# Moving the residual add of a graph-attention layer from VectorE to GpSimd, with a new order on all engines

## The chip, the cores and the metric

One core of a Trainium2 chip runs the whole program. The metric is the device time of one execution in microseconds (us). Five engines work side by side, each through its own instructions in order: TensorE (PE in the profile; its weight loads are PEld), VectorE (DVE), ScalarE (ACT), GpSimd (POOL) and SyncE (SP, which only issues DMAs here). They wait for each other through semaphores.

## The reference, cut to what matters

16 batches of 512 tokens with 128 features, in float32. First a graph-attention layer with a residual:

```
xn = layernorm(x);  Wh = xn @ W.T;  si = Wh @ a1;  sj = Wh @ a2
e = leaky_relu(si[:, None] + sj[None, :], 0.2);  att = softmax(where(adj > 0, e, -9e15))
x = x + elu(att @ Wh)
```

Then a second layernorm (to x2), a router that picks two of eight experts for each batch, two expert layers with a GELU between them, and a third layernorm. The second part begins when the token sums of all 16 batches are there.

## The kernel before, in words

A batch is four tiles (t = 0 to 3) of 128 rows. Up to about 180 us the kernel runs the attention stage: a software pipeline with one step for each batch n, two batches in a hardware loop. Each engine has its own hand-written `step(half, n)`, and this list sets its order of work; every engine works on several batches in one step. Most tiles have one buffer, so the batches are chained: `masked_dst`, `leaky`, `logit`, `h_att`, `h_exp`, the projection in PSUM and the shifts.

For one batch: TensorE transposes x (`transpose_x`), ScalarE copies it (`copy_xnt`), TensorE multiplies by W (`project`), and ScalarE scales the result by the first norm into `whx` (`copy_wh`), whose columns 0 and 1 hold sj and si. TensorE spreads sj over the partitions (`spread_dst`, L1408). VectorE adds the mask and takes row maxima (`masked_max`, four calls, L682). GpSimd works out row shifts from them (`row_shifts`, L502 to L513). ScalarE makes the leaky branch (`leaky_part`, L1150), VectorE takes the larger branch (`logits`, L694), TensorE transposes (`transpose_logits`, L1431), ScalarE takes the exponential (`probs`, L1180), TensorE multiplies by `whx` (`attend`, L1447). VectorE divides by the row sums (`invert_sums` L703, `normalize` L712), ScalarE takes exp(h) (`exp_h`, L1158), and VectorE forms x1 = max(h, 0) + x (`residual_pos`, L723) and x1 += min(exp(h), 1) (`residual_neg`, L731). The -1 of elu drops out of the later norm and is put back elsewhere.

The second norm: VectorE takes statistics (`stats2`, L741), GpSimd turns those of two batches at once, the first norm of batch n + 2 and the second norm of batch n - 3, into scales (`norms`, L461 to L490; `NORM_LAG` is 5), ScalarE applies them (`scale_x2`, L1191), TensorE transposes x2, ScalarE copies it (`copy_x2t`, L1198), and SP keeps x2 (`keep_x2`). `norms(n + 2)` may start only when `copy_wh(n)` has read the scales of the same buffer. SP loads rows and x; GpSimd issues the load of the adjacency matrix (`load_adj`, L436) once VectorE has made the mask out of the buffer (`make_mask`, L668). `waits_met(engine)` is a semaphore increment behind a wait.

Orders in step n before (function(batch), tile behind the comma):

```
DVE   max(n,2) pos(n-2) max(n,3) neg(n-2) stats2(n-2) stats1(n+3) mask(n+1) inv(n-1) logit(n,0) norm(n-1)
      logit(n,1) logit(n,2) max(n+1,0) max(n+1,1) logit(n,3)
ACT   xnt(n+1) scale_x2(n-3) leaky(n,0) leaky(n,1) wh(n+1) leaky(n,2) prob(n,0) x2t(n-3) leaky(n,3) prob(n,1)
      prob(n,2) exp_h(n-1) prob(n,3)
PE    x2(n-3) tl(n,0) spread(n+1) tl(n,1) tl(n,2) tx(n+2) att(n,0) tl(n,3) att(n,1) att(n,2) proj(n+2) att(n,3)
POOL  load_adj(n+2) norms(n+2) row_shifts(n)
```

The last three batches leave the loop and end in code of their own (`moments2_end`, `last_normalize`, `norm2_third_last` and others).

Of the kernel before, what the change touches and what calls it, by code (L numbers as in the profile page):

```python
# [10 lines left out]
ALU = mybir.AluOpType  # L11
# [17 lines left out]
def gat_moe_kernel(nc, x, adj, gnn_w, gnn_a, w_router, b_router, w1, b1, w2, b2, gamma, beta, out):  # L29
# [15 lines left out]
    with ExitStack() as ctx:  # L45
# [17 lines left out]
        minus_half = sb("minus_half", [P, T])  # L63
        gnn_w_sb = sb("gnn_w_sb", [P, D])
# [113 lines left out]
        s_x = [sem("x_loaded0"), sem("x_loaded1")]  # L178
        s_xr = [sem("x_rows_loaded0"), sem("x_rows_loaded1")]
# [32 lines left out]
        s_x1 = sem("x1_ready")  # L212
# [76 lines left out]
        V = 0  # L289
        NORM_LAG = 5  # L290
# [10 lines left out]

        def wait_x2(engine, half, b):
            engine.wait_ge(s_x2a, (T - V) * (b + 1))

# [4 lines left out]
        def _(sp):  # L309
# [19 lines left out]
            def keep_x2(half, n):  # L329
                b, h, par = batch_at(half, n)  # L330
                wait_x2(sp, half, b)
                waits_met(sp)
                sp.wait_ge(s_x1, 2 * b + 2)
                waits_met(sp)
                sp.dma_start(x_all[:, b, :], x2s[par][:]).then_inc(s_x2k[par], 16)
# [20 lines left out]
            def step(half, n):  # L356
                if in_range(half, n - 3, KEPT - 1):
                    keep_x2(half, n - 3)
                if isinstance(half, int) and 5 <= n + 5 < DIRECT:
                    load_direct(n + 5)  # L360
                if in_range(half, n + 4) and past(half, n + 4, DIRECT):
                    load_rows(half, n + 4)
                if in_range(half, n + 3) and past(half, n + 3, DIRECT):
                    load_x(half, n + 3)
# [55 lines left out]
        def _(pool):  # L420
# [16 lines left out]

            def norms(half, n):
# [14 lines left out]
                if second:  # L453
                    b2n = b - NORM_LAG
                    if past(half, b2n, 1):
                        pool.wait_ge(s_n2, 3 * b2n)
                    if past(half, b2n, 2):
                        pool.wait_ge(s_x2a, (T - V) * (b2n - 1))
                    pool.wait_ge(s_bn2, T * b2n + T)
# [32 lines left out]
            def row_shifts(half, n):  # L492


                b, h, par = batch_at(half, n)
                base, src = 7 * b, whx[par][:, :, 1]
                if past(half, b, 1):
                    pool.wait_ge(s_logit, T * b)
                    pool.wait_ge(s_leaky, T * b)
                pool.wait_ge(s_wh, T * b + T)  # L500
                waits_met(pool)
                nc.gpsimd.tensor_scalar(src_alpha[:], src, ALPHA, 0.0, ALU.mult, ALU.add).then_inc(s_shift, 1)  # L502
                pool.wait_ge(s_md, T * b + T)
# [4 lines left out]
                nc.gpsimd.tensor_scalar(z_pos[:], z_max[:], 0.0, 1.0 - ALPHA, ALU.max, ALU.mult).then_inc(s_shift, 1)  # L508
# [35 lines left out]
            def step(half, n):  # L544
                if in_range(half, n + 2) and past(half, n + 2, 2):
                    load_adj(half, n + 2)
# [87 lines left out]
        def _(dve):  # L634
            nc.vector.memset(ones[:], 1.0).then_inc(s_dconst, 1)
            for i in range(2):
                nc.vector.memset(whx[i][:], 1.0).then_inc(s_dconst, 1)

# [66 lines left out]
            def normalize(half, n):  # L705
                b, h, par = batch_at(half, n)
                if past(half, b, 1):
                    dve.wait_ge(s_hexp, b)
                    dve.wait_ge(s_x1, 2 * b - 1)
# [5 lines left out]
            def residual_pos(half, n):  # L715

                b, h, par = batch_at(half, n)
                dve.wait_ge(s_x[par], 16 * h + 16)
                if past(half, b, 1):
                    dve.wait_ge(s_x1, 2 * b)  # L720
# [5 lines left out]
            def residual_neg(half, n):  # L726
                b, h, par = batch_at(half, n)
                dve.wait_ge(s_hexp, b + 1)
                dve.wait_ge(s_x1, 2 * b + 1)
                waits_met(dve)  # L730
                nc.vector.scalar_tensor_tensor(out=x1_all[:, b, :], in0=h_exp[:], scalar=1.0, in1=x1_part[:],  # L731
                                               op0=ALU.min, op1=ALU.add).then_inc(s_x1, 1)

            def stats2(half, n):
                b, h, par = batch_at(half, n)
                dve.wait_ge(s_x1, 2 * b + 2)
# [3 lines left out]
                for t in range(T):  # L740
                    nc.vector.bn_stats(bn12[1 - par][:, 1, t, :],  # L741
                                       x1_all[:, b, t * D:(t + 1) * D]).then_inc(s_bn2, 1)

            def moments2_end(b, between=None):
                i = b - KEPT
                dve.wait_ge(s_x1, 2 * b + 2)
# [22 lines left out]
            def step(half, n):  # L769
                if in_range(half, n):  # L770
                    masked_max(half, n, 2)
                if in_range(half, n - 2, B - 2):
                    residual_pos(half, n - 2)
                if in_range(half, n):
                    masked_max(half, n, 3)
                if in_range(half, n - 2, B - 2):
                    residual_neg(half, n - 2)
                if in_range(half, n - 2, END - 1):
                    stats2(half, n - 2)
                if in_range(half, n + 3):  # L780
                    stats1(half, n + 3)
                if in_range(half, n + 1):
                    make_mask(half, n + 1)
                if in_range(half, n - 1, B - 2):
                    invert_sums(half, n - 1)
                if in_range(half, n):
                    logits(half, n, 0)
                if in_range(half, n - 1, B - 2):
                    normalize(half, n - 1)
                if in_range(half, n):  # L790
                    logits(half, n, 1)
# [46 lines left out]
            def residual_pos_pair(q):  # L838
                b, u, pair = B - 1, slice(2 * q, 2 * q + 2), slice(2 * q * D, (2 * q + 2) * D)
                if q == 0:  # L840
                    dve.wait_ge(s_x[1], 16 * (B // 2))
# [4 lines left out]
            def residual_neg_pair(q):  # L846
                b, pair = B - 1, slice(2 * q * D, (2 * q + 2) * D)
                dve.wait_ge(s_hexp, b + q + 1)
                dve.wait_ge(s_x1, 2 * b + 2 * q + 1)
# [3 lines left out]
            def moments2_last_pair(q, between=None):  # L853
                b = B - 1
                dve.wait_ge(s_x1, 2 * b + 2 * q + 2)
# [12 lines left out]
            residual_pos(0, B - 3)  # L868
            residual_neg(0, B - 3)
# [6 lines left out]
            residual_pos(0, B - 2)  # L876
            logits(0, B - 1, 3)
            residual_neg(0, B - 2)
# [240 lines left out]
        def _(act):  # L1119
# [8 lines left out]
            def copy_wh(half, n):  # L1128
# [11 lines left out]
                for t in range(T):  # L1140
                    nc.scalar.activation(whx[par][:, t, 0:D + 2], wh_ps[:, t, 0:D + 2], ACT.Copy,  # L1141
# [11 lines left out]
            def exp_h(half, n):  # L1153
                b, h, par = batch_at(half, n)
                act.wait_ge(s_hatt, T * b + T)
                if past(half, b, 1):
                    act.wait_ge(s_x1, 2 * b)
                nc.scalar.activation(h_exp[:], h_att[:].rearrange("p t d -> p (t d)"), ACT.Exp).then_inc(s_hexp, 1)  # L1158

            def last_normalize(t):  # L1160
                b = B - 1
                if t == 0:
                    act.wait_ge(s_hexp, b)
                    act.wait_ge(s_x1, 2 * b)
                act.wait_ge(s_inv, b + t + 1)
                nc.scalar.activation(h_att[:, t, :], last_av_ps[t][:, 0:D], ACT.Copy,
# [15 lines left out]
            def scale_x2(half, n):  # L1182
# [4 lines left out]
                act.wait_ge(s_x1, 2 * b + 2)  # L1187
                act.wait_ge(s_n2, 3 * b + 3)
                waits_met(act)
                for t in range(V, T):  # L1190
                    nc.scalar.activation(x2s[par][:, t * D:(t + 1) * D], x1_all[:, b, t * D:(t + 1) * D], ACT.Identity,  # L1191
                                         bias=nb2[1 - par][:, t:t + 1], scale=rstd12[1 - par][:, 1, t:t + 1]).then_inc(s_x2a, 1)
# [13 lines left out]
            def step(half, n):  # L1206
                if in_range(half, n + 1):
                    copy_xnt(half, n + 1)
                if in_range(half, n - 3, END - 1):
                    scale_x2(half, n - 3)  # L1210
# [10 lines left out]
                if in_range(half, n - 3, KEPT - 1):  # L1221
                    copy_x2t(half, n - 3)
                if in_range(half, n):
                    leaky_part(half, n, 3)
                if in_range(half, n):
# [3 lines left out]
                if in_range(half, n - 1, B - 2):  # L1229
                    exp_h(half, n - 1)  # L1230
# [21 lines left out]
            probs(0, 0, 1)  # L1252
            probs(0, 0, 2)
# [4 lines left out]
            def scale_x2_second_last():  # L1258
                act.wait_ge(s_x1, 2 * END + 2)
# [10 lines left out]
            scale_x2(0, B - 4)  # L1270
# [3 lines left out]
            probs(0, B - 1, 0)  # L1274
            leaky_part(0, B - 1, 3)
# [3 lines left out]
            copy_x2t(0, B - 4)  # L1279
# [3 lines left out]
            last_exp(0)  # L1283
            last_normalize(2)
# [77 lines left out]
        def _(pe):  # L1362
# [9 lines left out]
            def transpose_x(half, n):  # L1372
                b, h, par = batch_at(half, n)
                if in_range(half, n - 5):
                    pe.wait_ge(s_x2t, b - 4)
# [36 lines left out]
            def transpose_x2(half, n):  # L1412
                b, h, par = batch_at(half, n)
                wait_x2(pe, half, b)
                if in_range(half, n + 4):
                    pe.wait_ge(s_xt, b + 5)
# [34 lines left out]
            def step(half, n):  # L1451
                if in_range(half, n - 3, KEPT - 1):
                    transpose_x2(half, n - 3)
                if in_range(half, n):
                    transpose_logits(half, n, 0)
                if in_range(half, n + 1):
                    spread_dst(half, n + 1)
                if in_range(half, n):
                    transpose_logits(half, n, 1)
# [4 lines left out]
                if in_range(half, n):  # L1464
                    attend(half, n, 0)
                if in_range(half, n):
                    transpose_logits(half, n, 3)
                if in_range(half, n):
                    attend(half, n, 1)
                if in_range(half, n):  # L1470
                    attend(half, n, 2)
                if in_range(half, n + 2):
                    project(half, n + 2)
# [32 lines left out]
            transpose_x2(0, B - 4)  # L1506
# [7 lines left out]
            attend(0, B - 1, 3)  # L1514

# [168 lines left out]
```

## Time and profile before

| | |
|---|---|
| median of 3 runs | 299.86 us (299.11 to 301.21) |
| the profiled execution | 301.19 us, of which its span is 299.5 us |
| busy over the span | PE 264.6, DVE 242.4, ACT 230.1, POOL 164.2 us |
| attention stage | to about 180 us |

The span runs from the first to the last instruction; 1.7 us of the execution lie outside. A share of busy time over the whole span mixes two stages; the change touches the first.

### The profile page before, as it was taken

The numbers are of one execution on the slowest core, as the hardware profiler recorded it, in microseconds if no ns is written. First come the engines' busy times: TensorE is split into PE (matmuls) and PEld (weight loads), VectorE is DVE, ScalarE is ACT, GpSimd is POOL, SyncE is SP. The second block draws the span as 40 slices with busy tenths as digits, with TensorE's granted clock in tenths as the row PEclk, the third lists the DMA queues.
The fourth block names the chain that finished last, engine by engine and source line by source line (L and its number), as shares of the span: only waits on it lengthen the run. The fifth ranks groups of instructions, "written<-read, shape, count | busy, mean of one in ns | idle before, by whom it ended". The sixth has DMA issues, their size and how long they took to land. (4 is left out here: it accounts for less than half of the span.)

```text
span 299.5 us, 7855 instructions
## 1 busy us (share of the span) xinstructions
PE 264.6 (88%) x1958; PEld 238.8 (80%) x1959; DVE 242.4 (81%) x690; ACT 230.1 (77%) x498; POOL 164.2 (55%) x391
## 2 busy tenths in 40 slices
PE   7687879898889888988798798999999999999990
PEld 5477878898779777888797685689999999999980
DVE  4597989999999999999788967466678777688765
ACT  2367479888988898899879875778779887888570
POOL 3686575777667765776835851124343244332473
PEclk9979979999999999999989899999999999999997
DMA  6999343458457754776101000465464654646313
GB/s 106 177 292 172 56 73 57 113 79 178 85 129 141 145 120 120 140 175 137 45 0 37 35 1 20 163 209 158 147 192 155 213 168 156 188 158 204 92 37 105
DMA packets 47069, 37.26 MB, mean 124 GB/s; under 512 B 2848, under 2 KB 41152, under 8 KB 47040
## 3 DMA queue, kind: packets, MB, share of 16 engines
q1 hardware_dynamic: 38176, 27.49, 28.8%
q0 software_dynamic: 8864, 9.45, 21.4%
q8 instruction: 11, 0.18, 0.2%
q14 instruction: 18, 0.15, 0.1%
HBM read 29.57 MB, written 4.20 MB: 113 GB/s over the span
## 5 line engine op out<-in xcount | busy, mean ns | idle before, releaser
L1447 PE MATMUL banks<-whx,prob_t 128*128 128x129 f32 x512 | 65.6, 277 | 0.0
L1447 PEld LDWEIGHTS banks<-whx,prob_t 128*128 128x128 f32 x512 | 61.7, 194 | 0.0
L1431 PE MATMUL banks<-ident,logit 128*128 128x128 f32 x256 | 41.1, 297 | 18.2 <-DVE logit L694 17.2
L1431 PEld LDWEIGHTS banks<-ident,logit 128*128 128x128 f32 x256 | 30.7, 151 | 25.4 <-DVE logit L694 16.5
L1150 ACT ACTIVATE leaky<-masked_dst,shift_neg 128x512 f32<-128x512 f32 x64 | 44.4, 721 | 7.7 <-POOL shift_neg L512 7.7
L694 DVE SCALAR_TENSOR_TENSOR logit<-masked_dst,shift_pos,leaky 128x512 f32<-128x512 f32 x64 | 47.3, 749 | 3.1 <-ACT leaky L1150 2.6
L1180 ACT ACTIVATE prob_t<-banks 128x512 f32<-128x512 f32 x64 | 37.0, 604 | 13.2 <-PE banks L1431 13.1
L682 DVE CUSTOM_DVE_ANT_0 masked_dst<-mask,banks 128x512 f32<-128x512 bf16 x64 | 42.2, 682 | 2.5 <-PE banks L1408 1.6
L1316 ACT ACTIVATE logit<-logit,nb,rstd 128x128 f32<-128x128 f32 x60 | 24.8, 483 | 14.8 <-POOL nb L611 14.8
L606 POOL TENSOR_SCALAR veps<-mv 128x4 f32<-128x4 f32 x15 | 5.8, 387 | 48.9 <-DVE mv L1013 45.0
L1620 PEld LDWEIGHTS banks<-w2s,masked_dst 128*128 128x128 f32 x256 | 29.7, 192 | 1.1 <-issue 0.6
L1620 PE MATMUL banks<-w2s,masked_dst 128*128 128x128 f32 x256 | 30.0, 275 | 0.2 <-ACT w2s L1335 0.2
L1605 PE MATMUL banks<-x2t_hi,w_pair 128*128 128x512 f32 x64 | 26.8, 419 | 0.3 <-DMA w_pair<-w_parts 0.3
L1620 PEld LDWEIGHTS banks<-w2s,leaky 128*128 128x128 f32 x224 | 26.1, 192 | 0.6
L1620 PE MATMUL banks<-w2s,leaky 128*128 128x128 f32 x224 | 26.1, 275 | 0.0
L995 DVE TENSOR_TENSOR logit<-banks,x_all 128x512 f32<-128x512 f32 x15 | 10.4, 692 | 19.1 <-ACT logit L1316 12.7
L1607 PE MATMUL banks<-x2t_hi,w_pair 128*128 128x512 f32 x64 | 25.3, 395 | 0.0
L484 POOL TENSOR_TENSOR rstd<-sums,minus_half 128x8 f32<-128x8 f32 (+1 forms) x17 | 25.0, 1473 | 0.3
L1606 PE MATMUL banks<-x2t_lo,w_pair 128*128 128x512 f32 x64 | 24.9, 389 | 0.0
L1191 ACT ACTIVATE x2s<-x_all,nb,rstd 128x128 f32<-128x128 f32 (+1 forms) x52 | 21.4, 485 | 4.4 <-POOL nb L490 4.3
L436 POOL DMA_DIRECT2D adj_sb<-in_adj_dram x16 | 13.8, 861 | 19.0 <-DVE mask L668 18.3
L1408 PE MATMUL banks<-ident,whx 128*128 128x128 f32 x128 | 19.7, 301 | 2.9 <-ACT whx L1141 2.2
(171 smaller groups left out, 578.7 us busy)
## 6 DMA issues: line engine op xcount, KB each, us to landing
adj_sb<-in_adj_dram POOLq DMA_DIRECT2D x16, 512.0 KB, 5.9
w_pair<-w_parts SPq DMA_DIRECT2D x31, 256.0 KB, 2.7
x_all<-in_x_dram SPq DMA_DIRECT2D x16, 256.0 KB, 3.8
w2r<-in_L_ffn_W_dram SPq DMA_DIRECT2D x32, 128.0 KB, 2.2
out_dram<-prob_t SPq DMA_DIRECT2D x15, 256.0 KB, 2.3
x_all<-x2s SPq DMA_DIRECT2D x13, 256.0 KB, 2.3
x_rows<-in_x_dram SPq DMA_DIRECT2D x8, 256.0 KB, 3.0
w_parts<-in_L_ffn_W_dram SPq DMA_DIRECT2D x1, 1024.0 KB, 9.4
```

The costliest lines, as they stand in the source:

```text
L484: nc.gpsimd.tensor_tensor(rstd[:, kinds, :], sums[:, 1, kinds, :], minus_half[:].unsqueeze(1).to_broadcast([P, 2, T])[:, kinds, :], ALU.po ...
L682: nc.vector.tensor_tensor_reduce(out=masked_dst[:, t, :], in0=mask[:, t, :], in1=dst_ps, scale=1.0, scalar=-3e38, op0=ALU.add, op1=ALU.max ...
L694: nc.vector.scalar_tensor_tensor(out=logit[:, t, :], in0=masked_dst[:, t, :], scalar=shift_pos[:, t:t + 1], in1=leaky[:, t, :], op0=ALU.ad ...
L1150: nc.scalar.activation(leaky[:, t, :], masked_dst[:, t, :], ACT.Identity, bias=shift_neg[:, t:t + 1], scale=ALPHA).then_inc(s_leaky, 1)
L1180: nc.scalar.activation(prob_t[:, t, :], lt_ps[t % 2], ACT.Exp).then_inc(s_prob, 1)
L1316: nc.scalar.activation(zn[par][:, tile], zs[par][:, tile], ACT.Identity, bias=nb3[par][:, t:t + 1], scale=rstd3[par][:, t:t + 1]).then_inc ...
L1431: last = nc.tensor.transpose(lt_ps[t % 2][:, c * P:(c + 1) * P], logit[:, t, c * P:(c + 1) * P], ident[:])
L1447: last = nc.tensor.matmul(into[:, 0:D + 1], prob_t[:, t, c * P:(c + 1) * P], whx[par][:, c, 2:WHX], start=(c == 0), stop=(c == T - 1))
L1605: nc.tensor.matmul(hid_ps[kc], lo, x2t_hi[par][:], start=True, stop=False)
L1606: nc.tensor.matmul(hid_ps[kc], hi, x2t_lo[par][:], start=False, stop=False)
L1607: nc.tensor.matmul(hid_ps[kc], hi, x2t_hi[par][:], start=False, stop=True).then_inc(s_hid_ps, 1)
L1620: last = nc.tensor.matmul(y_ps[par][:, t * D:(t + 1) * D], hidden[par][:, kc, t * P:(t + 1) * P], w2s[par][:, kc // FC, kc % FC, :], start ...
```

## The change

What VectorE did in two calls, with x in the first, becomes one call on h + 1: elu(h) + 1 = max(h + 1, min(exp(h), 1)). ScalarE adds 1 to all columns of `whx`, so that attention gives h + 1 (its rows sum to 1); `exp_h` takes a bias of -1, and the constants in `row_shifts` make up for the 1 in si and sj. The add of x is a GpSimd call, `add_x`, for batches 0 to 12; for batches 13 and 14 it is a VectorE call; batch 15 goes as before, with -1 in `last_normalize`. Statistics, scaling, transposing and keeping of x2 come one step later, and `NORM_LAG` is 6. The orders change on every engine. In step n now:

```
DVE   max(n,2) max(n,3) elu_plus_one(n-2) stats2(n-3) stats1(n+3) mask(n+1) logit(n,0) inv(n-1) logit(n,1)
      norm(n-1) logit(n,2) max(n+1,0) max(n+1,1) logit(n,3)
ACT   leaky(n,0) leaky(n,1) wh(n+1) leaky(n,2) prob(n,0) x2t(n-4) leaky(n,3) exp_h(n-1) xnt(n+2) prob(n,1)
      prob(n,2) scale_x2(n-3) prob(n,3)
PE    x2(n-4) tl(n,0) tl(n,1) spread(n+1) tl(n,2) tx(n+2) att(n,0) proj(n+2) att(n,1) tl(n,3) att(n,2) att(n,3)
POOL  add_x(n-3) load_adj(n+2) norms(n+2) row_shifts(n)
```

The core of the diff:

```
+            def add_x(half, n):
+                b, h, par = batch_at(half, n)
+                pool.wait_ge(s_x[par], 16 * h + 16)
+                waits_met(pool)
+                pool.wait_ge(s_elu, b + 1)
+                waits_met(pool)
+                nc.gpsimd.tensor_tensor(x1_all[:, b, :], x1_all[:, b, :], x_all[:, b, :], ALU.add).then_inc(s_acc, 1)
...
-                nc.gpsimd.tensor_scalar(src_alpha[:], src, ALPHA, 0.0, ALU.mult, ALU.add).then_inc(s_shift, 1)
+                nc.gpsimd.tensor_scalar(src_alpha[:], src, ALPHA, 2.0 - 2.0 * ALPHA, ALU.mult, ALU.add).then_inc(s_shift, 1)
...
-                nc.vector.scalar_tensor_tensor(out=x1_part[:], in0=h_att[:].rearrange("p t d -> p (t d)"), scalar=0.0,
-                                               in1=x_all[:, b, :], op0=ALU.max, op1=ALU.add).then_inc(s_x1, 1)
...
-                nc.vector.scalar_tensor_tensor(out=x1_all[:, b, :], in0=h_exp[:], scalar=1.0, in1=x1_part[:],
-                                               op0=ALU.min, op1=ALU.add).then_inc(s_x1, 1)
+                nc.vector.scalar_tensor_tensor(out=x1_all[:, b, :], in0=h_exp[:], scalar=1.0,
+                                               in1=h_att[:].rearrange("p t d -> p (t d)"), op0=ALU.min,
+                                               op1=ALU.max).then_inc(s_elu, 1)
...
             def stats2(half, n):
-                dve.wait_ge(s_x1, 2 * b + 2)
+                dve.wait_ge(s_acc, b + 1)
...
-                    nc.scalar.activation(whx[par][:, t, 0:D + 2], wh_ps[:, t, 0:D + 2], ACT.Copy,
+                    nc.scalar.activation(whx[par][:, t, 0:D + 2], wh_ps[:, t, 0:D + 2], ACT.Copy, bias=1.0,
                                          scale=rstd12[par][:, 0, t:t + 1]).then_inc(s_wh, 1)
...
+                nc.scalar.activation(h_exp[:], h_att[:].rearrange("p t d -> p (t d)"), ACT.Exp,
+                                     bias=minus_one[:]).then_inc(s_hexp, 1)
```

In SP's step `keep_x2(n - 4)` stands in place of n - 3, with a wait for the transfer before it, and `load_x(n + 2)` in place of n + 3. In the end of the stage (last batch):

```
             masked_max(0, B - 1, 3)
-            residual_pos(0, B - 3)
-            residual_neg(0, B - 3)
+            stats2(0, B - 4)
+            elu_plus_one(0, B - 3)
+            add_x_end(B - 3)
             moments2_end(B - 3)
...
             probs(0, B - 1, 2)
-            copy_x2t(0, B - 4)
+            scale_x2(0, B - 4)
             last_normalize(0)
             probs(0, B - 1, 3)
             last_normalize(1)
             last_exp(0)
+            copy_x2t(0, B - 4)
             last_normalize(2)
             last_normalize(3)
...
             attend(0, B - 1, 3)
+            transpose_x2(0, B - 4)
```

## Rows read from the trace of the kernel before

**Rows 1.** The table by stage, 100 to 120 us: busy time of each engine

```profile
100.00:120.00 20.00, 17.71 (x149) 16.36 (x149) 19.08 (x51) 17.71 (x41) 13.61 (x37) 1.00 0.61 132
```

**Rows 2.** VectorE in order of time: start, duration, line, operation, shape, idle before

```profile
94.44 0.69 DVE L731 SCALAR_TENSOR_TENSOR x_all<-h_exp,x_part 128x512 f32 x1
...
102.90 0.69 DVE L723 SCALAR_TENSOR_TENSOR x_part<-h_att,x_all 128x512 f32<-128x512 f32 x1
103.50 0.68 DVE L682 CUSTOM_DVE_ANT_0 masked_dst<-mask,banks 128x512 f32<-128x512 bf16 x1
...
104.11 0.69 DVE L731 SCALAR_TENSOR_TENSOR x_all<-h_exp,x_part 128x512 f32 x1
...
105.88 0.87 DVE L659 BATCH_NORM_STATS2 bn<-x_rows 128x6 f32<-128x128 f32 x4
106.67 0.68 DVE L668 TENSOR_SCALAR mask<-adj_sb 128x2048 bf16<-128x2048 bf16 x1
...
107.35 0.75 DVE L694 SCALAR_TENSOR_TENSOR logit<-masked_dst,shift_pos,leaky 128x512 f32<-128x512 f32 x1
108.02 0.68 DVE L712 TENSOR_TENSOR h_att<-banks,inv_sum 128x512 f32<-128x512 f32 x1
...
114.29 0.69 DVE L731 SCALAR_TENSOR_TENSOR x_all<-h_exp,x_part 128x512 f32 x1
```

**Rows 3.** GpSimd in order of time, the same stretch

```profile
96.27 0.20 POOL L513 TENSOR_TENSOR shift_pos<-whx,row_max 128x4 f32<-128x4 f32 x1
...
102.40 1.67 POOL L484 TENSOR_TENSOR rstd<-sums,minus_half 128x8 f32<-128x8 f32 x1
104.22 0.63 POOL L490 TENSOR_TENSOR nb<-nm,rstd 128x4 f32<-128x4 f32 x1 [0.16 <-POOL rstd L484]
...
108.07 0.85 POOL L436 DMA_DIRECT2D adj_sb<-in_adj_dram  x1 [1.61 <-DVE mask L668]
109.47 0.20 POOL L461 TENSOR_TENSOR sums<-bn 128x8 f32<-128x8 f32 x1 [0.54 <-ACT whx L1141]
...
113.54 0.29 POOL L490 TENSOR_TENSOR nb<-nm,rstd 128x4 f32<-128x4 f32 x1 [0.16 <-POOL rstd L484]
```

**Rows 4.** ScalarE in order of time, the same stretch

```profile
103.12 0.60 ACT L1180 ACTIVATE prob_t<-banks 128x512 f32<-128x512 f32 x1 [0.47 <-PE banks L1431]
105.05 1.65 ACT L1191 ACTIVATE x2s<-x_all,nb,rstd 128x128 f32 x4 [0.86 <-POOL nb L490]
106.61 1.32 ACT L1150 ACTIVATE leaky<-masked_dst,shift_neg 128x512 f32<-128x512 f32 x2
```

**Rows 5.** VectorE and TensorE together, from one logit to the next maximum

```profile
97.83 0.72 DVE L694 SCALAR_TENSOR_TENSOR logit<-masked_dst,shift_pos,leaky 128x512 f32<-128x512 f32 x1
...
98.68 0.65 PE L1431 MATMUL banks<-ident,logit 128*128 128x128 f32 x4 [1.25 <-DVE logit L694]
...
99.17 1.06 PE L1408 MATMUL banks<-ident,whx 128*128 128x128 f32 x8
...
100.06 1.12 PE L1431 MATMUL banks<-ident,logit 128*128 128x128 f32 x8
...
100.41 0.69 DVE L682 CUSTOM_DVE_ANT_0 masked_dst<-mask,banks 128x512 f32<-128x512 bf16 x1
```

**Rows 6.** GpSimd's groups of instructions by shape, whole run: count, busy us, mean ns

```profile
L523 POOL TENSOR_SCALAR x_all<-x_all,mv,rstd 128x128 f32<-128x128 f32 x4 | 4.4, 1100 | 0.1
...
L578 POOL CAST w_pair<-w_parts 128x256 fp32r x2 | 0.7, 396 | 5.2 <-issue 5.2
```

**Rows 7.** GpSimd and VectorE in order of time, 168 us

```profile
168.44 0.81 POOL L523 TENSOR_SCALAR x_all<-x_all,mv,rstd 128x128 f32<-128x128 f32 x1
...
168.56 0.86 DVE L694 SCALAR_TENSOR_TENSOR logit<-masked_dst,shift_pos,leaky 128x512 f32<-128x512 f32 x1
```

**Rows 8.** TensorE and ScalarE in order of time, the end of the attention stage

```profile
173.39 2.85 PE L1447 MATMUL banks<-whx,prob_t 128*128 128x129 f32 x24
...
176.25 0.88 ACT L1166 ACTIVATE h_att<-banks,inv_sum 128x128 f32<-128x128 f32 x2 [0.74 <-DVE inv_sum L836]
```

More of the change, by code:

```diff
@@ L330, in keep_x2 @@
                 b, h, par = batch_at(half, n)
-                wait_x2(sp, half, b)
-                waits_met(sp)
-                sp.wait_ge(s_x1, 2 * b + 2)
+                if past(half, b, 2):
+                    sp.wait_ge(s_x2k[par], 16 * h)
+                    waits_met(sp)
+                sp.wait_ge(s_x2a, T * b + T)
                 waits_met(sp)
@@ L356, in step @@
             def step(half, n):
-                if in_range(half, n - 3, KEPT - 1):
-                    keep_x2(half, n - 3)
                 if isinstance(half, int) and 5 <= n + 5 < DIRECT:
                     load_direct(n + 5)
+                if in_range(half, n - 4, KEPT - 1):
+                    keep_x2(half, n - 4)
                 if in_range(half, n + 4) and past(half, n + 4, DIRECT):
                     load_rows(half, n + 4)
-                if in_range(half, n + 3) and past(half, n + 3, DIRECT):
-                    load_x(half, n + 3)
+                if in_range(half, n + 2) and past(half, n + 2, DIRECT):
+                    load_x(half, n + 2)
             step(0, -1)
@@ L544, in step @@
             def step(half, n):
-                if in_range(half, n + 2) and past(half, n + 2, 2):
+                if in_range(half, n - 3, KEPT - 1):
+                    add_x(half, n - 3)
+                if in_range(half, n + 2) and past(half, n + 2, 3):
                     load_adj(half, n + 2)
@@ L783, in step @@
                     make_mask(half, n + 1)
+                if in_range(half, n):
+                    logits(half, n, 0)
                 if in_range(half, n - 1, B - 2):
@@ L786, in step @@
                 if in_range(half, n):
-                    logits(half, n, 0)
+                    logits(half, n, 1)
                 if in_range(half, n - 1, B - 2):
                     normalize(half, n - 1)
-                if in_range(half, n):
-                    logits(half, n, 1)
                 if in_range(half, n):
@@ L867, in _ @@
             masked_max(0, B - 1, 3)
-            residual_pos(0, B - 3)
-            residual_neg(0, B - 3)
+            stats2(0, B - 4)
+            elu_plus_one(0, B - 3)
+            add_x_end(B - 3)
             moments2_end(B - 3)
@@ L875, in _ @@
             logits(0, B - 1, 2)
-            residual_pos(0, B - 2)
             logits(0, B - 1, 3)
-            residual_neg(0, B - 2)
+            elu_plus_one(0, B - 2)
+            add_x_end(B - 2)
             invert_tile(0)
@@ L1220, in step @@
                     probs(half, n, 0)
-                if in_range(half, n - 3, KEPT - 1):
-                    copy_x2t(half, n - 3)
+                if in_range(half, n - 4, KEPT - 1):
+                    copy_x2t(half, n - 4)
                 if in_range(half, n):
                     leaky_part(half, n, 3)
+                if in_range(half, n - 1, B - 2):
+                    exp_h(half, n - 1)
+                if in_range(half, n + 2):
+                    copy_xnt(half, n + 2)
                 if in_range(half, n):
@@ L1228, in step @@
                     probs(half, n, 2)
-                if in_range(half, n - 1, B - 2):
-                    exp_h(half, n - 1)
+                if in_range(half, n - 3, KEPT - 1):
+                    scale_x2(half, n - 3)
                 if in_range(half, n):
@@ L1274, in _ @@
             probs(0, B - 1, 0)
+            copy_x2t(0, B - 5)
             leaky_part(0, B - 1, 3)
@@ L1278, in _ @@
             probs(0, B - 1, 2)
-            copy_x2t(0, B - 4)
+            scale_x2(0, B - 4)
             last_normalize(0)
@@ L1283, in _ @@
             last_exp(0)
+            copy_x2t(0, B - 4)
             last_normalize(2)
@@ L1373, in transpose_x @@
                 b, h, par = batch_at(half, n)
-                if in_range(half, n - 5):
-                    pe.wait_ge(s_x2t, b - 4)
+                if in_range(half, n - 6):
+                    pe.wait_ge(s_x2t, b - 5)
                 if past(half, b, 1):
@@ L1413, in transpose_x2 @@
                 b, h, par = batch_at(half, n)
[L1414 to L1416 removed]
+                pe.wait_ge(s_x2a, T * b + T)
+                if in_range(half, n + 5):
+                    pe.wait_ge(s_xt, b + 6)
                 elif isinstance(half, int):
@@ L1465, in step @@
                     attend(half, n, 0)
+                if in_range(half, n + 2):
+                    project(half, n + 2)
+                if in_range(half, n):
+                    attend(half, n, 1)
                 if in_range(half, n):
```

88 lines of the change are left out of this document (39 added, 49 removed).

## The prediction

> **What bounds the kernel now.** I read the table by stage first: in the middle of the attention stage VectorE is busy 19.08 of 20 us, TensorE and ScalarE 17.7 each, GpSimd 13.6 [rows 1]. VectorE is nearly full, so the next view is its order of time. One step there is the distance between two like calls: from L731 at 94.44 to the one at 114.29 are two steps, 19.85 us, so 9.92 us a step [rows 2]. Calls follow each other a little sooner than they last; what counts is start to start: 0.60 for a residual call, 0.61 for a maximum, 0.79 for four statistics, 0.68 for mask and reciprocal together, 0.67 for a logit [rows 2], and by the same overlap 0.60 for `normalize`. Before the change that is 2 x 0.60 + 4 x 0.61 + 2 x 0.79 + 0.68 + 4 x 0.67 + 0.60 = 9.18 us, and 0.74 us of gaps.
>
> The other views show what these gaps hang on. Two rings run close behind VectorE. The first: after the last maximum (the next call starts at 94.44) GpSimd works out the shifts and is done at 96.27 + 0.20 = 96.47, 2.03 us later [rows 2, 3]; then come leaky, logit, and VectorE again. The second: GpSimd's norms from 109.47 to 113.54 + 0.29 = 113.83 take 4.36 us; ScalarE starts the x2 scaling 0.20 us behind their end (104.85 to 105.05), the leaky calls 1.56 later, and the next norms start 2.86 us after these (106.61 to 109.47), released by the copy of `whx` [rows 3, 4]. That ring is 4.62 + 4.36 = 8.98 us, and each norm call that is held up by VectorE makes it longer: the last of the chain takes 0.63 us beside L731 at 104.11, and 0.29 us at 113.54, before L731 starts at 114.29 [rows 2, 3]. Three such calls make 10.0. So the stage is bound by VectorE, with this ring at its heels; a call less on VectorE is worth its 0.60 only if nothing else is put in.
>
> **The change part by part.** *VectorE's calls.* One 512-column call of 0.60 us leaves each step: 8.58 us remain. The gap between the residual call and its statistics goes as well, since those are now one step older. I leave 0.2 us for small gaps: 8.8.
>
> *The order on TensorE.* `spread_dst(n+1)` now stands behind the second logit transpose, and `masked_max(n+1, 0)` waits for it. TensorE begins a transpose 0.85 us after the start of its logit (97.83 to 98.68), goes on to the next item 0.49 later, the spread takes 0.89 to the next start, and the maximum starts 0.35 after that [rows 5]: from the start of logit 1 to the maximum are now 0.85 + 0.49 + 0.89 + 0.35 = 2.58 us. VectorE has in that time logit 1, `normalize` and logit 2, 0.67 + 0.60 + 0.67 = 1.94. So a new wait of 0.64 us appears in each step, as long as the call that was saved. Before, the spread stood one transpose earlier and the maximum came with no gap. Behind the waiting maximum stand the rest of VectorE's step, and behind these all others. VectorE's step is then 9.45 us if GpSimd's add costs it nothing: 0.47 less than now.
>
> *The add on GpSimd.* No row shows a two-input call of 512 columns there. Nearest: a cast of 256 columns takes 396 ns [rows 6]; less the 0.20 that a call of four columns takes [rows 3], 0.77 ns a column, so 0.6 us for 512 columns of one input and 1.0 for two. Against it, calls of 128 columns beside VectorE's logits took 1.1 us each [rows 6], which for four times the columns is 4.4. I take 1.0, since the higher figure is time spent waiting. On GpSimd it lies where that engine waited 1.61 us for the mask [rows 3], so GpSimd itself has room. What matters is what it does to VectorE. Where one GpSimd call of 128 columns had begun 0.12 us before a logit, the logit took 0.86 instead of 0.75 us [rows 2, 7]; eight times that (four times the columns, two inputs) is 0.9. GpSimd starts the add when the shifts are done, 2.03 us behind the last maximum, plus up to 0.2 for two waits. VectorE is then at 0.60 + 0.79 + 0.79 = 2.18: the statistics, which read one input, are just over, and the mask and the logits follow. So nearly all of the add falls on calls that it can hold up. I take 0.95 us a step for VectorE; the bounds are 0 (the calls take turns in the gaps) and 1.1. That makes 9.45 + 0.95 = 10.40 us a step.
>
> The Trainium skill ("SBUF — State Buffer", Who interferes with whom) says that a VectorE call with two SBUF inputs, or in a two-port mode, and a GpSimd call that reads SBUF block each other fully, whoever starts first. The slow calls in [rows 3, 7] agree. But the power call at 102.40 lasts 1.67 us, over the residual call at 102.90 that takes its usual 0.69 [rows 2, 3]: the hold is the time of reading, not of the whole call. For the length of the add the Trainium skill ("GPSIMD Engine Reference", Elementwise — side-by-side cycle accounting) gives about 2.6 cycles an element at 1.2 GHz, an estimate of 1.1 us here; by it the sum below would be 2 us higher.
>
> *The order on ScalarE.* `scale_x2` waits for the norms as before, but `probs(n, 3)` now stands between it and the next leaky. The second ring gets 0.5 us longer: 0.20 + 1.56 + 0.5 + 2.86 = 5.12, and with norms of 4.36 to 5.4 us 9.5 to 10.5. The added biases cost at most some hundredths each. This ring alone eats what VectorE would gain when two or more norm calls are held up.
>
> *GpSimd's queue.* `load_adj` stands behind the add and goes out up to 1.5 us later; its mask is due a step later, so that is hidden while the load lands within a step. `keep_x2` and `load_x` on SP are moved by a step; what reads them stands four steps behind the load. The norm lag costs nothing: the buffers alternate as before.
>
> *Head and end.* In the first two steps the new wait is there and no call has gone: 2 x 0.3 = 0.6 us. At the end the transposes of x2 for batch 12 stand behind the last attend, whose group ends at 173.39 + 2.85 = 176.24, and `copy_x2t` stands before `last_normalize(2)`, which started at 176.25 [rows 8]: four transposes of 0.65 [rows 5], 0.2 to wake ScalarE, a copy of 0.60 (the size of the probability call at 103.12 [rows 4]) are 1.45 us, on the path of the last batch to the token sums. Statistics of batch 12 and `add_x_end` fit where VectorE waits for the last attends. Bounds: 0.8 and 2.5, since `norms` for batch 12 now comes after the last shifts and pushes GpSimd's closing norms.
>
> *Sum.* (10.40 - 9.92) x 13 steps with an add = 6.2; plus 0.6, plus 1.5: 8.3 us. The profiled execution took 301.19 us (span 299.5 and 1.7 around it) and would take 309.5; it is 1.3 above the median, so the forecast from 299.86 is 308.2 us.
>
> **The rivals.** *GpSimd's add does not hold VectorE* (reads slip into the gaps, as with the power call). The step is 9.45: -0.47 x 13 + 2.1 = -4.0, so 295.9 us. For it: VectorE's loss in [rows 7] is small. Against: 0.11 for 128 columns already, and eight times the reading here. This is the other side, and it decides where the add costs VectorE under 0.3 us a step. Chance 0.20.
>
> *The add is half absorbed.* If it slips behind the mask and logit 0 and lands beside `normalize`, what it holds up is logit 2, and the new wait of 0.64 behind that swallows most. Loss 0.35, step 9.8: -0.12 x 13 + 2.1 = +0.5, 300.4 us. For it: the start of the add and of the mask are within 0.2 us, and order decides. Chance 0.16.
>
> *The ScalarE ring takes over.* If the mask is pushed to end 3.9 us behind the last maximum, the adjacency load starts 0.7 later (mask at 106.67 + 0.68, load at 108.07) and takes 0.85 [rows 2, 3], the norms start at 5.5, last 4.4 to 5.4, and with 0.20 + 1.56 + 0.5 the next leaky is at 12.2 to 13.2, where the shifts alone would want it 2.03 us behind the next maximum: a step of 10.1 to 11.1. At 10.9: +0.98 x 13 + 2.1 = 14.8, 314.7 us. Chance 0.18.
>
> **How the numbers follow.** The forecast has chance 0.46 and a range of its own of 304 to 312 (the add at 0.6 to 1.1, the end at 0.8 to 2.5). A measurement here tells about 1%, 3 us. Faster by over 1% is the first rival less what of it lies near the line: 0.19; within 1% the second: 0.17; slower the forecast and the third: 0.64. The range from 296 to 313.5 us leaves out about half of the first rival and half of the third.
>
> **What would show it.** In the profile after: the distance between two elu calls (10.4 us is the forecast; 9.45 the first rival); an idle time of 0.6 to 0.9 us before the first of four maxima, released by TensorE L1408's successor; the add at 1.0 to 1.1 us and a mask or a logit 0 that lasts longer or starts later by 0.9 to 1.0; idle ScalarE before `scale_x2`, and leaky released by ScalarE's own order, not by GpSimd; at the end `last_normalize(2)` some 1.4 us behind the last attend. The prediction is wrong if the mask and logit 0 stay at their length and place beside the add, or if TensorE's spread is ready when the maximum wants it.

## The result, and the profile after

The changed kernel takes 308.68 us (median of 6 runs, 307.05 to 309.68), the kernel before beside it 300.13: a ratio of 1.029 (95% interval 1.026 to 1.032). The forecast was 308.2. The profiled execution has a span of 307.8 us, 8.3 more than before.

VectorE in order of time (start, duration, line, operation, shape, idle before), to be held against [rows 2]. L733 is `elu_plus_one`, L749 `stats2`, L680 the mask, L706 a logit, L694 a maximum:

```profile
98.33 0.69 DVE L733 SCALAR_TENSOR_TENSOR x_all<-h_exp,h_att 128x512 f32 x1
98.94 0.87 DVE L749 BATCH_NORM_STATS2 bn<-x_all 128x6 f32 x4
99.72 0.86 DVE L671 BATCH_NORM_STATS2 bn<-x_rows 128x6 f32<-128x128 f32 x4
100.49 0.68 DVE L680 TENSOR_SCALAR mask<-adj_sb 128x2048 bf16<-128x2048 bf16 x1
101.22 1.62 DVE L706 SCALAR_TENSOR_TENSOR logit<-masked_dst,shift_pos,leaky 128x512 f32<-128x512 f32 x1
...
102.86 0.71 DVE L706 SCALAR_TENSOR_TENSOR logit<-masked_dst,shift_pos,leaky 128x512 f32<-128x512 f32 x1
103.50 0.68 DVE L724 TENSOR_TENSOR h_att<-banks,inv_sum 128x512 f32<-128x512 f32 x1
104.10 0.74 DVE L706 SCALAR_TENSOR_TENSOR logit<-masked_dst,shift_pos,leaky 128x512 f32<-128x512 f32 x1
106.29 0.69 DVE L694 CUSTOM_DVE_ANT_0 masked_dst<-mask,banks 128x512 f32<-128x512 bf16 x1 [1.46 <-issue]
```

GpSimd beside it, to be held against [rows 3]; L445 is the add:

```profile
100.17 0.20 POOL L522 TENSOR_TENSOR shift_pos<-whx,row_max 128x4 f32<-128x4 f32 x1
100.51 1.78 POOL L445 TENSOR_TENSOR x_all<-x_all  x1
102.24 0.86 POOL L436 DMA_DIRECT2D adj_sb<-in_adj_dram  x1
103.29 0.35 POOL L470 TENSOR_TENSOR sums<-bn 128x8 f32<-128x8 f32 x1 [0.19 <-issue]
...
107.44 0.20 POOL L499 TENSOR_TENSOR nb<-nm,rstd 128x4 f32<-128x4 f32 x1 [0.16 <-POOL rstd L493]
```

The add is issued at 100.51, beside the mask, ends at 102.29, and the logit behind the mask lasts 1.62 us instead of 0.75: it was held until 102.09 (its end at 102.84 less 0.75), when the add was nearly done. In other steps the add comes first and the mask is held. One line for each kind of step, the mask or logit from VectorE's view and the add from GpSimd's:

```profile
49.41 1.65 DVE L680 TENSOR_SCALAR mask<-adj_sb 128x2048 bf16<-128x2048 bf16 x1
...
90.71 1.75 DVE L706 SCALAR_TENSOR_TENSOR logit<-masked_dst,shift_pos,leaky 128x512 f32<-128x512 f32 x1
```

```profile
49.24 1.27 POOL L445 TENSOR_TENSOR x_all<-x_all 128x512 f32<-128x512 f32 x1
```

Alone the add takes 1.27 us; 1.78 is 1.27 and 0.51 of waiting for the mask. The other new cost is the idle time before the first maximum: 1.46 us at 106.29, and 0.53 to 0.78 in the other steps between 60 and 140 us. The 1.46 are no fair sample: TensorE had stood idle for the held logit, and its granted clock was 0.50 from 104.0 to 107.1, where the spread took 1.92 us, against 1.06 at full clock.

```profile
102.97 1.43 PE L1443 MATMUL banks<-ident,logit 128*128 128x128 f32 x8 [1.72 <-DVE logit L706]
```

"Issue" means that the view names no releaser, and three of these waits it puts down to ScalarE's leaky call; but the only leaky call that this maximum waits for, that of tile 0 one batch earlier, is long over. The spread on TensorE (L1420) is what stands there, and the experiments bear it out.

How long is a step? The first and the thirteenth `elu_plus_one` of the changed kernel, then the same calls of the kernel before:

```profile
36.67 0.69 DVE L733 SCALAR_TENSOR_TENSOR x_all<-h_exp,h_att 128x512 f32<-128x512 f32 x1
...
160.94 0.69 DVE L733 SCALAR_TENSOR_TENSOR x_all<-h_exp,h_att 128x512 f32<-128x512 f32 x1
```

```profile
35.23 0.69 DVE L731 SCALAR_TENSOR_TENSOR x_all<-h_exp,x_part 128x512 f32<-128x512 f32 x1
...
154.72 0.69 DVE L731 SCALAR_TENSOR_TENSOR x_all<-h_exp,x_part 128x512 f32<-128x512 f32 x1
```

124.27 / 12 = 10.36 us a step against 119.49 / 12 = 9.96. The 8.3 us of span are: 1.4 by the first such call, 4.8 in these 12 steps, 0.6 in the next one (10.84 against 10.20), 0.7 from there to the sums for the router (189.12 - 171.78 against 181.54 - 164.92), and 0.8 behind them.

### The profile page after: what moved, and what is told of

Its sections match the earlier page's. It is cut to its first block and busy times, and to the rows that moved or that the text cites. A ratio compares the mean times of both kernels' runs of the same rounds, so it can differ in the third digit from the quotient of the medians.

```text
span 307.8 us, 7857 instructions
## 1 busy us (share of the span) xinstructions
PE 265.6 (86%) x1958; PEld 240.8 (78%) x1959; DVE 242.5 (79%) x678; ACT 232.5 (76%) x498; POOL 181.2 (59%) x411
## 3 DMA queue, kind: packets, MB, share of 16 engines
q0 software_dynamic: 8864, 9.45, 20.3%
## 5 line engine op out<-in xcount | busy, mean ns | idle before, releaser
L1459 PE MATMUL banks<-whx,prob_t 128*128 128x129 f32 x512 | 68.0, 279 | 0.8 <-ACT prob_t L1190 0.4
L1459 PEld LDWEIGHTS banks<-whx,prob_t 128*128 128x128 f32 x512 | 62.9, 194 | 2.2 <-ACT prob_t L1190 2.0
L1443 PE MATMUL banks<-ident,logit 128*128 128x128 f32 x256 | 42.6, 294 | 25.4 <-DVE logit L706 23.9
L706 DVE SCALAR_TENSOR_TENSOR logit<-masked_dst,shift_pos,leaky 128x512 f32<-128x512 f32 x64 | 53.6, 840 | 6.9 <-POOL shift_pos L522 3.6
L694 DVE CUSTOM_DVE_ANT_0 masked_dst<-mask,banks 128x512 f32<-128x512 bf16 x64 | 41.2, 683 | 11.4 <-issue 7.4
L617 POOL TENSOR_SCALAR veps<-mv 128x4 f32<-128x4 f32 x15 | 7.0, 468 | 47.9 <-DVE mv L1020 43.8
L1338 ACT ACTIVATE masked_dst<-banks,b_sel 128x512 f32<-128x512 f32 x32 | 19.7, 678 | 3.3 <-PE banks L1620 2.6
L1420 PE MATMUL banks<-ident,whx 128*128 128x128 f32 x128 | 20.0, 307 | 2.4 <-ACT whx L1148 2.4
```

The source lines that it names most:

```text
L694: nc.vector.tensor_tensor_reduce(out=masked_dst[:, t, :], in0=mask[:, t, :], in1=dst_ps, scale=1.0, scalar=-3e38, op0=ALU.add, op1=ALU.max ...
L706: nc.vector.scalar_tensor_tensor(out=logit[:, t, :], in0=masked_dst[:, t, :], scalar=shift_pos[:, t:t + 1], in1=leaky[:, t, :], op0=ALU.ad ...
L1443: last = nc.tensor.transpose(lt_ps[t % 2][:, c * P:(c + 1) * P], logit[:, t, c * P:(c + 1) * P], ident[:])
L1459: last = nc.tensor.matmul(into[:, 0:D + 1], prob_t[:, t, c * P:(c + 1) * P], whx[par][:, c, 2:WHX], start=(c == 0), stop=(c == T - 1))
```

## The experiments

"Step" is the mean of the same 12 distances in each profile. Ratios are to the kernel before, run beside each, with a 95% interval. In e2, e3, e9, e12 and e15 the result of the kernel lacks x in batches 0 to 12; they are there for their times alone.

| run | step, us | median, us | ratio and interval |
|---|---|---|---|
| kernel before | 9.96 | 300.1 | |
| changed kernel | 10.36 | 308.68 | 1.029 (1.026 to 1.032) |
| e1, spread early | 9.62 | 300.06 | 1.002 (0.998 to 1.007) |
| e2, add of 4 columns | 9.80 | 301.33 | 1.002 (0.998 to 1.005) |
| e3, both | 9.62 | 300.90 | 0.999 (0.995 to 1.004) |
| e5, before with the spread late | 10.86 | 312.67 | 1.042 (1.035 to 1.049) |
| e6, add ahead of the shifts | 10.22 | 307.78 | 1.030 (1.023 to 1.037) |
| e9, e3 and scale_x2 last | 10.15 | 305.93 | 1.024 (1.018 to 1.030) |
| e10, e1 and mask ahead of stats1 | 9.59 | 298.87 | 0.999 (0.995 to 1.003) |
| e11, e10, normalize early, scale_x2 last | 10.34 | 307.32 | 1.026 (1.021 to 1.030) |
| e12, e9 with TensorE's order of before | 9.59 | 299.81 | 0.998 (0.994 to 1.002) |
| e13, e10 with that order, scale_x2 last | 9.62 | 298.04 | 0.994 (0.990 to 0.998) |
| e14, e13 and normalize early | 10.38 | 309.32 | 1.030 (1.026 to 1.034) |
| e15, GpSimd only writes | 9.82 | 301.16 | 1.006 (1.002 to 1.009) |

**e1, the spread back in its place.**

```
-                if in_range(half, n):
-                    transpose_logits(half, n, 1)
                 if in_range(half, n + 1):
                     spread_dst(half, n + 1)
+                if in_range(half, n):
+                    transpose_logits(half, n, 1)
```

> The changed kernel with spread_dst(n+1) put back between the first and the second logit transpose on TensorE. Theory of two costs (the spread makes the first maximum wait 0.64 us a step, the add holds VectorE 0.95 us a step): the step goes from 10.36 to about 9.7 us, 308.7 - 0.64 x 13 = 300.4 us. Rival, the add alone is the cost and the wait for the spread only fills time that was lost anyway: under 2 us gained, 307 or more. Rival, the ring of norms, scale_x2, probs and leaky sets the step: it stays at 10.0 or more, 304 or more.

The spread and the second transpose trade places, and 8.6 us are gone; both rivals fall. Putting the spread back regains all that the changed kernel lost in time. The step is even 0.34 us shorter than in the kernel before, but the time is the same. In the profiled execution most of that lead is lost between the last `elu_plus_one` and the router's sums (see the last section); for the other executions no trace was kept.

**e2, the add cut to four columns.**

```
-                nc.gpsimd.tensor_tensor(x1_all[:, b, :], x1_all[:, b, :], x_all[:, b, :], ALU.add).then_inc(s_acc, 1)
+                nc.gpsimd.tensor_tensor(x1_all[:, b, 0:4], x1_all[:, b, 0:4], x_all[:, b, 0:4], ALU.add).then_inc(s_acc, 1)
```

> The changed kernel with GpSimd's add cut from 512 to 4 columns, so x is missing from nearly all of x1 in batches 0 to 12; every wait and the order stay. Theory of two costs: the mask and logit 0 take their usual 0.68 and 0.75 us, the step goes to about 9.45 us, 308.7 - 0.95 x 13 = 296.4 us. Rival, the ring on ScalarE: the step stops at 9.8 to 10.0, 301 to 304. Rival, the spread alone is the cost: 307 or more.

No logit is held any more (the longest of 64 is 0.81 us, before the edit 1.76), and 7.4 us are gone. So the hold was real, and either cost alone was worth nearly the whole loss. But the mean step is 9.80, not 9.45: something else lies right beneath.

**e3, both edits.**

> Both edits in one: spread early, and GpSimd's add cut to 4 columns (x is missing from nearly all of x1 in batches 0 to 12). If the two costs simply add up, the step is 8.8 us and the time 308.7 - 8.3 - 12.3 = 288. If the ScalarE ring of 5.12 us plus norms of 4.4 lies beneath (9.5 us), it stops at about 297, no better than the add cut alone; then scale_x2 waits idle for the norms and leaky starts straight behind probs(n-1, 3).

In the mean the costs do not add: with both gone the step is that of e1 alone. But the mean mixes two kinds of steps. Batches 4 to 9 are in the hardware loop (from the 5th `elu_plus_one` to the 11th), and there the changed kernel, e1, e2 and e3 need 10.48, 9.77, 10.03 and 10.15 us a step. In the three steps ahead of it (from the 2nd call to the 5th) they need 10.20, 9.51, 9.21 and 8.93. There the two costs come off nearly one by one, and the 8.8 of my sum are nearly reached. VectorE's calls in e3, one step ahead of the loop and one in it, with ScalarE and the logit of the latter between:

```profile
44.34 0.69 DVE L733 SCALAR_TENSOR_TENSOR x_all<-h_exp,h_att 128x512 f32<-128x512 f32 x1
53.22 0.69 DVE L733 SCALAR_TENSOR_TENSOR x_all<-h_exp,h_att 128x512 f32<-128x512 f32 x1
...
101.33 0.69 DVE L733 SCALAR_TENSOR_TENSOR x_all<-h_exp,h_att 128x512 f32 x1
102.45 1.65 ACT L1201 ACTIVATE x2s<-x_all,nb,rstd 128x128 f32 x4 [1.25 <-POOL nb L499]
104.48 1.32 ACT L1157 ACTIVATE leaky<-masked_dst,shift_neg 128x512 f32<-128x512 f32 x2
105.22 0.75 DVE L706 SCALAR_TENSOR_TENSOR logit<-masked_dst,shift_pos,leaky 128x512 f32<-128x512 f32 x1 [0.88 <-ACT leaky L1157]
...
111.94 0.69 DVE L733 SCALAR_TENSOR_TENSOR x_all<-h_exp,h_att 128x512 f32 x1
```

In the loop `scale_x2` waits idle for the norms, leaky starts straight behind `probs(n-1, 3)`, and logit 0 waits for leaky: the ring that the expectation names. The norms take 4.83 us there (97.42 to 102.25), 3.93 ahead of the loop (48.81 to 52.74). Why the loop makes them longer is not shown.

**e5, the late spread in the kernel before.** The edit of e1 reversed, in the old kernel.

> The kernel before, with only spread_dst(n+1) put behind the second logit transpose. In the kernel before normalize stands between logit 0 and logit 1, so from logit 1 VectorE needs only two logits, 1.34 us, to the first maximum, against 2.58 on TensorE: a wait of up to 1.2 us a step. Theory of two costs: 300.1 + (0.64 to 1.2) x 14 = 309 to 317 us. Rival, the late spread costs nothing by itself: 300 to 302.

The clearest single test. VectorE's maximum now names its releaser:

```profile
98.84 0.69 DVE L682 CUSTOM_DVE_ANT_0 masked_dst<-mask,banks 128x512 f32<-128x512 bf16 x1 [1.36 <-PE banks L1408]
```

1.36 us idle, against 1.24 by the working of [rows 5]; 0.90 of it stay in the step.

**e15, a GpSimd call that reads nothing.** The add becomes `nc.gpsimd.memset(x1_part[:], 0.0)`, behind a wait for the memset before it.

> The changed kernel with GpSimd's add replaced by a memset of 512 columns of a buffer that is not in use (x is missing in batches 0 to 12), at the same place in the order: GpSimd is busy there and writes 512 columns, but reads nothing. Theory that it is the reading that holds VectorE: the logits behind it take their usual 0.75 us, the step is as with the add of 4 columns, 9.8 us, 300 to 302 us. Rival, any GpSimd call of some length in that place holds mask and logits or delays the queue behind it: logits or masks of 1.2 us and more, 304 to 308 us.

```profile
76.11 0.67 DVE L683 TENSOR_SCALAR mask<-adj_sb 128x2048 bf16<-128x2048 bf16 x1
...
76.26 0.99 POOL L448 MEMSET x_part<- 128x512 f32 x1
...
76.99 0.75 DVE L709 SCALAR_TENSOR_TENSOR logit<-masked_dst,shift_pos,leaky 128x512 f32<-128x512 f32 x1 [0.20 <-ACT leaky L1160]
```

The memset takes 0.52 us alone; here it lasts 0.99, to 0.47 behind the mask's end at 76.78: the mask holds a call that only writes, too. The logit at 76.99 runs its 0.75 us while the memset is still on until 77.25. So this logit is not held by a busy GpSimd that only writes; what is left for the add is its reading. As a test of length it is weak: the memset is less than half of the add, and only 0.26 us of it lie beside the logit.

**e6, the add between norms and shifts.** On GpSimd `add_x(half, n - 3)` goes behind `norms(half, n + 2)`.

> The changed kernel with add_x moved on GpSimd from behind the shifts to between norms and shifts, where VectorE runs maxima, which read one SBUF input. Theory that place decides the hold: mask and logit 0 take their usual 0.68 and 0.75 us. But the shifts now wait for the add: it starts when norms and logit 3 are done, about 1.2 us ahead of the last maximum's end, and ends about when the shifts are wanted; if that fits, the step is 9.5 to 9.8 us, 298 to 302. Rival, the add delays the shifts by most of its 1.27 us: the step stays at 10.2 to 10.5 and the time at 306 to 310.

```profile
96.77 1.80 DVE L733 SCALAR_TENSOR_TENSOR x_all<-h_exp,h_att 128x512 f32 x1
...
109.34 0.87 DVE L749 BATCH_NORM_STATS2 bn<-x_all 128x6 f32 x4 [1.37 <-POOL x_all L445]
```

The rival was right. Mask and logit 0 have their usual length, but now `elu_plus_one` is held for 1.1 us, or the statistics wait for the add itself, and the shifts are late.

**e10, statistics beside the add.** On VectorE `make_mask(half, n + 1)` goes ahead of `stats1(half, n + 3)`, on top of e1.

> The changed kernel with the early spread (9.62 us a step, 300.1 us), and on VectorE the mask ahead of stats1 instead of behind it, so that when the shifts are done and the add starts, VectorE is at statistics that read one input. Theory of the hold: about 0.6 of the 1.27 us of the add is covered, logit 0 is held for 0.5 instead of 1 us, less some 0.2 for shifts that the mask holds up: 0.2 to 0.5 us a step, 294 to 297. Rival, the ring on ScalarE is the bound at 9.5 to 9.6: 299 to 301.

```profile
74.98 0.67 DVE L680 TENSOR_SCALAR mask<-adj_sb 128x2048 bf16<-128x2048 bf16 x1
75.01 0.70 POOL L519 TENSOR_TENSOR row_max<-z_pos,z_alpha 128x4 f32<-128x4 f32 x1
...
76.28 1.28 POOL L445 TENSOR_TENSOR x_all<-x_all  x1
...
76.99 1.12 DVE L706 SCALAR_TENSOR_TENSOR logit<-masked_dst,shift_pos,leaky 128x512 f32<-128x512 f32 x1 [0.55 <-ACT leaky L1157]
```

The hold is down to 0.37 us here (0.30 to 0.59 in ten of the 12 steps, still 0.90 and 0.96 in two), but the mask now holds the shifts (0.70 us for a call of 0.20), leaky is late, and logit 0 waits 0.55 for it. The step stays, and the time is the rival's. Its cause is not shown by that: in this step leaky waits for the shifts, not for ScalarE's own order.

**e9 and e12, which ring lies beneath.** On ScalarE `scale_x2(half, n - 3)` goes behind `probs(half, n, 3)`; e12 also has TensorE's whole step in the order of before.

> The kernel with both costs taken out (spread early, GpSimd's add cut to 4 columns, x missing in batches 0 to 12) stood at 9.62 us a step, not at 8.8. Here scale_x2(n-3) also goes behind probs(n, 3) on ScalarE. Theory that the ring of norms, scale_x2, probs, leaky and whx sets that step: the ring loses 0.5 us or more, the step goes to 8.9 to 9.1 us, 291 to 293 us. Rival, something else holds the 9.62 us (GpSimd's queue with the adjacency load, row loads): no gain, 299 or more.

My theory failed: 0.53 us a step slower. ScalarE shows why:

```profile
95.59 0.60 ACT L1190 ACTIVATE prob_t<-banks 128x512 f32<-128x512 f32 x1 [1.67 <-PE banks L1443]
...
96.09 1.64 ACT L1201 ACTIVATE x2s<-x_all,nb,rstd 128x128 f32 x4
```

In the changed order of TensorE the last transpose stands behind `project` and attend 1. Probs 3 waits 1.67 us for it, and `scale_x2` and the next leaky now stand behind that wait.

> The kernel with spread early and the add at 4 columns (x missing in batches 0 to 12), scale_x2 behind probs(n, 3), and now TensorE's whole step in the order of the kernel before, so that transpose_logits(n, 3) stands ahead of attend 1, attend 2 and project. With scale_x2 behind probs 3 and the changed order the step had grown to 10.15 us, and ScalarE waited 1.7 us for that transpose. Theory that the place of that transpose is what probs 3, and with it scale_x2, waited for: the wait goes, the ring is 4.62 us plus norms, the step 8.9 to 9.2 us, 290 to 293 us. Rival, the adjacency load and the copy of whx that GpSimd waits for set the step: 9.6 or more, 299 or more.

The long wait is gone, but the mean step is 9.59, no better than e3. Again it mixes: ahead of the loop the step is 9.35 (e3 8.93), in the loop 9.82 (e3 10.15). GpSimd, ScalarE and VectorE at the same place:

```profile
84.73 0.74 POOL L521 TENSOR_TENSOR shift_neg<-src_alpha,row_max 128x4 f32<-128x4 f32 x1
84.74 0.67 DVE L680 TENSOR_SCALAR mask<-adj_sb 128x2048 bf16<-128x2048 bf16 x1
85.50 1.34 ACT L1157 ACTIVATE leaky<-masked_dst,shift_neg 128x512 f32<-128x512 f32 x2 [0.39 <-POOL shift_neg L521]
86.26 0.75 DVE L706 SCALAR_TENSOR_TENSOR logit<-masked_dst,shift_pos,leaky 128x512 f32<-128x512 f32 x1 [0.85 <-ACT leaky L1157]
...
88.40 0.20 POOL L470 TENSOR_TENSOR sums<-bn 128x8 f32<-128x8 f32 x1 [1.17 <-ACT whx L1148]
```

So in the loop the place of `scale_x2` was worth 0.33 us a step, and beneath it lies the same ring by its other branch. The last maximum is over at 82.58, but GpSimd begins the shifts only at 83.43, behind its norms (until 83.26); leaky waits for the shifts, `copy_wh` stands behind leaky, and the next norms wait for `copy_wh`. From norms to norms these are 9.92 us (78.48 to 88.40). VectorE's calls make it longer: the shift beside the mask takes 0.74 us for 0.20. That is read from the rows; no run takes this ring away.

**e13, the best full kernel**, and **e11 and e14**, with `invert_sums` and `normalize` ahead of logit 0.

> A full kernel: the changed one with TensorE's step in the order of before, the mask ahead of stats1 on VectorE and scale_x2 behind probs(n, 3). Theory: the hold is about 0.4 us a step, VectorE's calls 8.6, gaps 0.2, ring of 9.0: step 9.2 to 9.3, 294 to 296 us. Rival, no room left beside the ring: 9.6, 299.

298.04 us: 0.6% under the kernel before, and 3.4% under the changed one. Its step is no shorter than that of e1, and its time is not clear of that of e10. The steps of 9.2 to 9.3 of the theory are not reached.

> As the kernel with early spread and mask ahead of stats1, and more: invert_sums and normalize(n-1) ahead of logit 0, so that VectorE has 1.5 us of calls with one SBUF input while GpSimd adds, and scale_x2(n-3) behind probs(n, 3) on ScalarE. Theory of hold plus ring: the add is hidden, the step is bound by VectorE's 8.6 us of calls and some gaps, or the ring of 9.0: 9.0 to 9.2 us a step, 291 to 294 us. Rival, the ring or the waits for the last attend hold it at 9.6: 300.

> As the one with mask early, transposes early and scale_x2 last, and invert_sums and normalize(n-1) ahead of logit 0. Theory: the add of 1.27 us is all beside statistics and normalize, no call is held; VectorE's step 8.8 to 9.1 us, 291 to 294 us. Rival, normalize waits for the last attend or logit 0 comes so late that TensorE and ScalarE behind it set the step: 9.5 to 10, 298 to 303.

Both are worse. e11 has e9's wait for the last transpose as well. In e14 no call of VectorE is held (the add takes its 1.27 us in each step), but VectorE waits for the last attend of the batch before, then for its own reciprocal, and logit 0 begins 2.3 us behind leaky (88.86):

```profile
90.12 0.18 DVE L715 RECIPROCAL inv_sum<-banks 128x4 f32<-128x4 f32 x1 [0.85 <-PE banks L1459]
...
90.55 0.69 DVE L724 TENSOR_TENSOR h_att<-banks,inv_sum 128x512 f32<-128x512 f32 x1 [0.25 <-DVE inv_sum L715]
...
91.16 2.07 DVE L706 SCALAR_TENSOR_TENSOR logit<-masked_dst,shift_pos,leaky 128x512 f32<-128x512 f32 x3
```

## Why the prediction was right

The time, the sign and both mechanisms were right. That the time was met to 0.5 us is in part luck: the steps gave 0.8 us less than forecast, the head 0.8 more.

- *The step*: 10.40 forecast, 10.36 measured (9.92 taken for before, 9.96 measured). Over 13 steps 5.4 us for the 6.2 of the sum, and some 0.9 us of the 5.4 are the one step at the lower clock (11.06, against 10.12 and 10.14 for the like steps two before and two after it), which the sum does not have.
- *The spread*: 0.64 forecast, 0.53 to 0.78 measured, and the step fell by 0.74 when it was put back (e1). The new wait is, as forecast, "as long as the call that was saved".
- *The hold*: 0.95 forecast; in ten steps logit 0 was held for 0.86 to 1.01 (1.61 and 1.76 less 0.75) or the mask for 0.97 to 1.03, in the first and the last two logit 0 for only 0.30. The add itself took 1.27 us, not the 1.0 from the cast of [rows 6]. The Trainium skill's rule on calls that block each other ("SBUF — State Buffer", Who interferes with whom) holds here for mask and logits, and e15 agrees that a call of two SBUF inputs is not held by one that only writes. The Trainium skill's 2.6 cycles an element ("GPSIMD Engine Reference", Elementwise — side-by-side cycle accounting), an estimate of 1.1 us, were nearer than my 1.0. By that estimate the sum would have been 1.4 us higher (0.11 in 13 steps), not 2 as the prediction has it.
- *Not seen*: the sum of VectorE's calls, gaps and waits holds ahead of the loop (10.20, 9.21 and 8.93 measured for 10.40, 9.45 and 8.8), but not in it once a cost is gone. The first rival, "GpSimd's add does not hold VectorE", was priced at a step of 9.45 and 295.9 us; e2 takes the hold away and gives 9.80 and 301.33. Had that condition come true, the price would have been wrong by 5 us, because it leaves out the second ring, which the prediction itself had put at 9.5 to 10.5 us.
- *The ScalarE ring*, as a rival of its own: in the changed kernel leaky was released by the shifts (seven of the waits, 3.6 us, lie between 60 and 140 us), so it did not take over. With the hold gone it did (e3).
- *Head*: 0.6 forecast, 1.4 measured by the first `elu_plus_one`. It is not shown that the spread causes it: e2, with the late spread, has that call at 35.21, as early as the kernel before. *End*: 1.5 forecast for `last_normalize(2)`. It starts 1.06 us behind the last attends, against 0.01 in the kernel before [rows 8]:

```profile
180.06 2.97 PE L1459 MATMUL banks<-whx,prob_t 128*128 128x129 f32 x24
...
184.09 0.62 ACT L1176 ACTIVATE h_att<-banks,inv_sum 128x128 f32<-128x128 f32 x2
```

From the `elu_plus_one` at 171.78 to the router's sums only 0.7 us are lost. What the 0.8 behind the sums are, no run tells.

## What to carry to other kernels

Count what stands between a producer and its consumer on both engines before trading two neighbours: one transpose moved ahead of the spread cost 0.7 us in every step, more than the 0.6 of the call that was saved. In these runs the add on GpSimd held no call of VectorE beside statistics and `normalize`, which read one SBUF input (e14); beside the mask or a two-input call it cost 0.86 to 1.03 us of its 1.27 where most of it lay beside them, whichever came first. When one cost is taken out, price the next bound by a chain through all engines, not by the sum of the busiest one. And look at the steps one by one before believing their mean: here it hid two kinds of steps, and with them both the success and the failure of the sum.

## What the runs showed of the hardware

In the profiled execution of e1 the granted clock of TensorE falls at 176.1 us, in the short stage ahead of the second part (table by stage: busy time and calls of PE, PEld, DVE, ACT and POOL, then the clock, third from last):

```profile
175.00:180.00 5.00, 4.30 (x20) 3.60 (x21) 2.55 (x10) 2.79 (x7) 1.20 (x4) 0.61 0.01 2
180.00:185.00 5.00, 4.59 (x20) 3.05 (x21) 2.47 (x16) 1.48 (x6) 0.00 (x0) 0.50 0.02 3
```

0.50 is 1.2 GHz, the lower of its two levels. Before the fall TensorE had stood idle from 174.96 to 175.70. In e10 it stood idle as long at the same place (174.74 to 175.49), and the clock stayed at 1.00. The router's sums come 2.4 us later in e1 than in e10, counted from the last `elu_plus_one` of the pipeline (180.72 - 167.93 against 178.50 - 168.13), while their steps are alike. So 2.4 us of a profile can be the clock in a stage that the edit does not touch; the profiles of e2, e3 and e15 show the same 0.50, those of e12 and e13 do not. Whether the order of the engines has a part in it stays open: the executions of e1 alone took 299.0 to 303.0 us, those below 301 us at mean granted clocks of 0.980 to 0.987, the others at 0.958 to 0.971.
